# Input tiles turned in 32-blocks on VectorE and placed by DMA copies, low parts on GpSimd, maxima scores over 128 rows

## The chip, the cores and the metric

The kernel runs on one NeuronCore of a Trainium2 chip. The metric is device time in microseconds of one execution; the median of three runs is compared. The engines are TensorE (PE: matrix products into PSUM; PEld is its loading of the stationary operand), VectorE (DVE), ScalarE (ACT), GpSimd (POOL) and SyncE (SP), which here only issues DMAs. Each engine works through its own list in order, and semaphores tie the lists together. All DMAs of this kernel's main part are issued by SP.

## The reference

Cross-attention over 32 batches. Queries and context are both 512 x 512, there are 16 heads of 32.

```
qn  = layer_norm(q)  * g_q + b_q          # q = x[b],  512 x 512
kvn = layer_norm(kv) * g_k + b_k          # kv = ctx[b], 512 x 512
Q, K, V = qn @ Wq, kvn @ Wk, kvn @ Wv     # 16 heads of 32
attn = softmax(Q K^T / sqrt(32))
ctx  = attn V
out  = q + gelu(ctx @ Wo + bo)
```

## The kernel before

The accuracy is that of fp32, reached by splitting each operand of the large products into a high part (rounded to the type fp32r by a ScalarE copy) and a low part (what is left), and adding three products: high by high, high by low, low by high. So each 512-wide product of the projections takes 12 matrix instructions of 512 columns (L856), and one plan token of PE (`q`, `k`, `v`, `o`) stands for two of them.

A batch is worked in four steps; a step holds one unit, that is four heads. The loop `batch(b)` of every engine walks the same four steps, and what each engine does in a step, and in which order, is written out by hand in the table `ORDER` (`st*3` means three tokens `st`). In step s of batch b the kernel works on several units at once:

- `st` (L876): the 16 transposed score products of unit s, out of `k_stack` and `q_stack`; ScalarE turns each into `probs` by Exp (L563).
- `s` (L883): the 16 score products of unit s+1, only to find each row's maximum; VectorE reduces each (L706). They use the first 96 of the 128 rows of the stacks (`KROWS`), which hold high and low parts of Q and K one above the other. Rows 96 to 127 of `q_stack` take the negated maxima (`mx`, L617, which follows `m`, `mh`, `ml`), and those of `k_stack` a mask of heads, so that `st` subtracts the maxima.
- `q`, `k` (L856): the projections of unit s+2. ScalarE writes their high part and VectorE their low part into `q_nat` and `k_nat` (L594, L608, L688), and SP copies them into the stacks by `restack`: three DMAs of 256 KB each for q (`rq`) and three for k (`rk`), each from 128 partitions to 32 partitions. The stacks have two slots, so these copies wait on the semaphore `stack_used`, which the first matrix instruction of the first `pv` block after the last `st` raises. The first `s` of the next step waits for all six to have landed.
- `pv` (L903): two blocks of probabilities times V per step; `z` (L847): row sums over `probs`, after GpSimd has added the four chunks (`add`, L475, six per step); then VectorE's `zt zr zb cn` and the `split` of the context into `ctx_hl`.
- Once per batch: `v` and `o` projections, and the preparation of the next batch's eight input tiles (four of x, four of ctx, each 128 tokens x 512). A tile is loaded (`load`), its mean and variance are taken (`ln`, `la`, `lv`), ScalarE normalises it in place (`norm`, L584), PE transposes it with four 128 x 128 instructions into a PSUM bank (`x`, L943), ScalarE copies the high part to `xT` or `cT` (L588) and VectorE subtracts to get the low part (L686).

Before the first batch, a head (b = -1) prepares weights, biases and the first tiles.

## Time and profile before

| | |
|---|---|
| median of 3 runs | 3265.43 us (3265.21 to 3265.64) |
| profiled execution, its own time | 3262.8 us |
| its span | 3261.0 us |
| PE busy | 3230.8 us, 99% |
| DVE, ACT, POOL busy | 69%, 70%, 71% |
| DMA engines, mean busy share | about 60% |
| granted TensorE clock, mean | 0.998 |

The span is the time between first and last instruction of that one execution; the difference of 1.8 us to its own time lies around it. Of the page, the busy shares say who could bound, and the chain that ended last says who did: it is followed back from the last instruction through whatever released each step. The timeline of one engine shows single instructions, with the idle time in front of one in brackets.

### The profile page before, as it was taken

Reading aid. Unit: us, or ns where it says so; the run is one execution under the profiler, and the core shown is the slowest. Engines: PE = TensorE matmul, PEld = TensorE weight load, DVE = VectorE, ACT = ScalarE, POOL = GpSimd, SP = SyncE. Lnnn points to the kernel's source line nnn. Section 1 sums busy time; section 2 is a strip of 40 time slices with the busy share of each in tenths; the row PEclk is TensorE's granted clock in tenths of the full one; section 3 lists DMA queues with packets and bytes.
Section 4 is the critical chain, followed back from the end, with each engine's and each line's share of the span. In section 5 each row is a group of like instructions: output and inputs, shape, how many; then the busy total and the mean of one; then the engine's idle time right before and its main releaser. Section 6 shows DMA issues by size and latency. Waiting matters only on the chain.

```text
span 3261.0 us, 49855 instructions
## 1 busy us (share of the span) xinstructions
PE 3230.8 (99%) x16611; PEld 2135.1 (65%) x16611; DVE 2256.9 (69%) x4769; ACT 2280.3 (70%) x3985; POOL 2313.9 (71%) x1544
## 2 busy tenths in 40 slices
PE   8999999999999999999999999999999999999998
PEld 5566666666666666666666666666666666666664
DVE  6667667676676676666766766766667767667664
ACT  5677666777767777667767667776777676677765
POOL 3676776777677767777776677777767776777765
PEclk9999999999999999999999999999999999999999
DMA  5655656566556656565665566665656655666653
GB/s 142 87 108 107 108 104 116 91 111 107 107 104 104 111 107 107 104 118 89 111 109 106 105 102 111 109 104 104 120 86 112 107 107 107 100 111 108 105 79 76
DMA packets 186721, 343.02 MB, mean 105 GB/s; under 512 B 20561, under 2 KB 20577, under 8 KB 186466
## 3 DMA queue, kind: packets, MB, share of 16 engines
q1 hardware_dynamic: 186000, 339.03, 60.0%
q8 instruction: 134, 2.20, 0.3%
q10 hardware_dynamic: 466, 0.80, 0.2%
q14 instruction: 121, 0.99, 0.1%
HBM read 104.87 MB, written 33.55 MB: 42 GB/s over the span
## 4 chain that ended last, share of the span: by engine, by line
PE 97%; DVE 1%; ACT 1%; issue 1%; DMA 0%; POOL 0%; SPq 0%; ACTq 0%; POOLq 0%; DVEq 0%
PE gen L856 43%; PE score L883 16%; PE score L876 15%; PE ctx L903 14%; PE gen L847 4%; PE gen L943 4%; PE gen L965 1%; DVE maxes L706 1%; DMA k_stack<-k_nat 0%; ACT q_stack L617 0%; PE score L788 0%; ACT probs L563 0%; DVE stats L725 0%; PE gen L837 0%; POOL probs L475 0%
## 5 line engine op out<-in xcount | busy, mean ns | idle before, releaser
L475 POOL TENSOR_TENSOR probs<-probs 128x1024 f32<-128x1024 f32 x762 | 1800.3, 2392 | 287.8 <-PE ctx L903 281.6
L706 DVE TENSOR_REDUCE maxes<-score 128x1 f32<-128x512 f32 x2048 | 1294.9, 680 | 217.5 <-PE score L883 213.9
L563 ACT ACTIVATE probs<-score 128x512 f32<-128x512 f32 x2048 | 1090.2, 621 | 141.1 <-PE score L876 137.5
L883 PE MATMUL score<-k_stack,q_stack 96*128 96x512 f32 x2048 | 761.2, 413 | 3.3 <-DVE maxes L706 1.8
L876 PE MATMUL score<-q_stack,k_stack 128*128 128x512 f32 x2048 | 696.4, 406 | 6.6 <-ACT q_stack L617 6.5
L883 PEld LDWEIGHTS score<-k_stack,q_stack 96*128 96x128 f32 x2048 | 378.2, 188 | 221.3 <-ACT probs L563 83.6
L876 PEld LDWEIGHTS score<-q_stack,k_stack 128*128 128x128 f32 x2048 | 374.7, 188 | 199.9 <-DVE maxes L706 64.4
L903 PE MATMUL ctx<-probs,v_sb 128*32 128x512 f32 x4096 | 492.5, 598 | 0.0
L856 PE MATMUL gen<-cT,w_k 128*128 128x512 f32 x1536 | 461.7, 400 | 0.2 <-DVE q_nat L688 0.2
L856 PE MATMUL gen<-w_v,cT 128*128 128x512 f32 x1536 | 461.4, 395 | 0.0
L856 PE MATMUL gen<-xT,w_q 128*128 128x512 f32 x1536 | 447.9, 394 | 0.0
L856 PE MATMUL gen<-w_o,ctx_hl 128*128 128x512 f32 x1488 | 416.4, 396 | 0.0
L491 POOL TENSOR_TENSOR rstd<-var_eps,minus_half 128x1 f32<-128x1 f32 x256 | 140.5, 549 | 335.0 <-DVE neg_mean L737 333.1
L502 POOL TENSOR_TENSOR ctx_hl<-ctx_n,ctx_hl 128x512 fp32r<-128x512 f32 x128 | 164.2, 1283 | 290.4 <-ACT ctx_hl L569 290.4
L617 ACT ACTIVATE q_stack<-max_hl,chunk_mask 32x512 fp32r<-32x512 f32 x512 | 326.3, 706 | 42.3 <-DVE max_hl L771 41.5
L856 PEld LDWEIGHTS gen<-w_v,cT 128*128 128x128 f32 x1536 | 287.3, 189 | 84.1 <-issue 26.8
L856 PEld LDWEIGHTS gen<-xT,w_q 128*128 128x128 f32 x1536 | 288.5, 190 | 60.6
L856 PEld LDWEIGHTS gen<-cT,w_k 128*128 128x128 f32 x1536 | 287.5, 192 | 55.2 <-DVE q_nat L688 1.1
L688 DVE SCALAR_TENSOR_TENSOR k_nat<-gen,bias_k,k_nat 128x512 fp32r<-128x512 f32 x128 | 95.8, 748 | 318.0 <-ACT k_nat L608 318.0
L856 PEld LDWEIGHTS gen<-w_o,ctx_hl 128*128 128x128 f32 x1488 | 276.7, 189 | 57.3
L903 PEld LDWEIGHTS ctx<-probs,v_sb 128*32 128x32 f32 x4096 | 106.9, 109 | 233.8 <-issue 233.8
L574 ACT ACTIVATE v_sb<-gen 128x512 f32<-128x512 f32 x128 | 76.5, 598 | 255.1 <-PE gen L856 255.1
(89 smaller groups left out, 2765.4 us busy)
## 6 DMA issues: line engine op xcount, KB each, us to landing
k_stack<-k_nat SPq DMA_DIRECT2D x384, 256.0 KB, 7.6
q_stack<-q_nat SPq DMA_DIRECT2D x381, 256.0 KB, 5.6
tok<-in_x SPq DMA_DIRECT2D x132, 256.0 KB, 11.0
tok<-in_ctx SPq DMA_DIRECT2D x128, 256.0 KB, 12.0
res<-in_x SPq DMA_DIRECT2D x124, 256.0 KB, 2.7
out<-res SPq DMA_DIRECT2D x124, 256.0 KB, 2.1
probs<-in_L_xattn_Wq SPq DMA_DIRECT2D x1, 1024.0 KB, 8.2
probs<-in_L_xattn_Wk SPq DMA_DIRECT2D x1, 1024.0 KB, 10.4
```

The lines of the kernel that those rows point to most:

```text
L475: pool.tensor_tensor(probs[:, c + 1, heads], probs[:, c + 1, heads], probs[:, c, heads], ALU.add).then_inc(pool_added, 1)
L491: pool.tensor_tensor(rstd[:, n:n + 1], var_eps[:, n:n + 1], minus_half[:], ALU.pow).then_inc(ln_rstd, 1)
L502: pool.tensor_tensor(ctx_hl[:, 1, up], ctx_n[:], raw(ctx_hl[:, 0, up]), ALU.subtract).then_inc(ctx_split, 1)
L563: act.activation(probs[:, n, part, :], score_at(s, "st", i)[:], ACT.Exp, scale=SCALE).then_inc(exp_done, 1)
L617: act.activation(q_stack[SROW:P, u1 % 2, :, P * n:P * (n + 1)], raw(max_hl[SROW:P, :]).unsqueeze(1).to_broadcast([SHIFTS, HU, P]), ACT.Ide ...
L706: dve.tensor_reduce(maxes[:, u1 % 2, SROW + i:SROW + i + 1], score_at(s, "s", i)[:], AX_X, ALU.max, negate=True).then_inc(max_done, 1)
L847: mm = pe.matmul(bank[DH * j:DH * (j + 1), :], ones[:, 0:DH], probs[:, c, j, :], start=(i == 0), stop=(i == len(chunks) - 1))
L856: mm = pe.matmul(bank[:, :], stationary(hs, c), moving(hm, c), start=(i == 0), stop=(i == len(TERMS) * NC - 1))
L876: pe.matmul(score_bank(pe, b, s, "st", i)[:, :], k_stack[:, s % 2, part, P * n:P * (n + 1)], q_stack[:, s % 2, part, :], start=True, stop= ...
L883: pe.matmul(score_bank(pe, b, s, "s", i)[:, :], q_stack[0:KROWS, u1 % 2, n, P * part:P * (part + 1)], k_stack[0:KROWS, u1 % 2, n, :], star ...
L903: mm = pe.matmul(ctx_ps[DH * j:DH * (j + 1), :], v_sb[:, c, lo:lo + DH], probs[:, c, j, :], start=(c == 0), stop=(c == NC - 1))
L943: mm = pe.matmul(bank[:, P * c:P * (c + 1)], tok[:, n, P * c:P * (c + 1)], ident[:], start=True, stop=True, is_transpose=True)
```

## The change

The transposing of the input tiles leaves PE, for all batches but the first (whose tiles are still transposed on PE in the head). A tile is now loaded so that partition 32g+j holds token 128g+32t+j for tile t. VectorE turns it in blocks of 32 x 32 (`xt`, one 128 x 512 transpose per tile) into `turned_tok`; 16 DMAs of 64 KB for the four tiles of x and 16 for those of ctx (`xd`, four per token) copy the blocks into the low half of `xT` or `cT`, from 32 partitions to 32 partitions. ScalarE reads them there and writes the high half (`x`), and GpSimd subtracts in place to leave the low half (`x` in the list of GpSimd; on VectorE only in the head, `xl`). `tok` shrinks to four tiles.

The `s` products run over all 128 rows. For that rows 96 to 127 of the `q_stack` slot must be zero, so each `rq` now begins with a DMA of 256 KB of zeros from DRAM, which waits for `stack_used`; PE's first `s` waits for it too (`rows_cleared`).

All five tables of `ORDER` are new. The core of the diff (of the tables the lines of SP alone):

```diff
-        "load*8 rq rk store res",
-        "rq rk store res store",
-        "store first_res rk rq first_res",
-        "rq rk",
+        "load*5 rq rk",
+        "load*3 xd*4 rq rk store xd*2 res xd*2",
+        "store res store rk rq store first_res*2",
+        "rk rq",
...
+    zero_rows = nc.dram_tensor("zero_rows", (SHIFTS, HU * D), F32).ap()
...
-        tok = sb("tok", [P, 2 * NC, D])
+        tok = sb("tok", [P, NC, D])
+        turned_tok = sb("turned_tok", [P, NC, NC, NC, DH])
...
+                if (b, s) == (-1, 0):
+                    for i in range(2 * NC):
+                        load_tile(0, i)
                 if (b, s) == (-1, 1):
+                    sp.wait_ge(act_out_free, 1)
+                    sp.dma_start(zero_rows.rearrange("r (c n) -> (r c) n", n=D), act_out[:]).then_inc(zeros_stored, 16)
...
-                if valid(b - 1):
-                    wait(sp, full["x"], 8 * (b - 1) + i + 1)
-                src = x_v[NC * b + i] if i < NC else c_v[NC * b + i - NC]
-                sp.dma_start(tok[:, i, :], src).then_inc(tile_loaded[i], 16)
+                if known(b) and b == 1 and i < NC:
+                    wait(sp, full["x"], i + 1)
+                elif not known(b) or b > 0:
+                    wait(sp, tok_turned, 8 * b + i - 11)
+                src, n = (x_v, i) if i < NC else (c_v, i - NC)
+                if known(b) and b == 0:
+                    sp.dma_start(tile(b, i), src[n]).then_inc(tile_loaded[i], 16)
+                else:
+                    src = src.rearrange("(b n) p d -> b (n p) d", n=NC)[b]
+                    sp.dma_start(tile(b, i), src.rearrange("(g t j) d -> t g j d", g=NC, t=NC)[n]).then_inc(tile_loaded[i], 16)
+
+            def spread_tile(b, n):
+
+                which, g = "c" if n >= NC else "x", n % NC
+                if g == 0:
+                    wait(sp, tok_turned, 8 * (b - 1) + n + NC)
+                    if which == "x":
+                        wait(sp, full["q"], NU * b)
+                    else:
+                        wait(sp, full["k"], NU * b)
+                        wait(sp, full["v"], NC * b)
+                for m in range(NC):
+                    sp.dma_start(raw(xt[which][DH * m:DH * (m + 1), 1, g, :, :]),
+                                 turned_tok[DH * g:DH * (g + 1), m, :, :, :].rearrange("p c t j -> p c (t j)")
+                                 ).then_inc(x_landed[g], 16)
...
+                        if kind == "xd" and valid(b) and valid(b + 1):
+                            spread_tile(b + 1, n)
+                        if kind == "rq" and valid(b2):
+                            if known(b) and (b, s) == (-1, 2):
+                                sp.wait_ge(zeros_stored, 16)
+                            wait(sp, stack_used, NU * b2 + u2 + 1)
+                            sp.dma_start(raw(q_stack[SROW:P, u2 % 2, :, :]),
+                                         zero_rows.rearrange("r (c n) -> r c n", n=D)).then_inc(rows_cleared[u2 % 2], 16)
-                            wait(sp, stack_used, NU * b2 + u2 + 1)
                             if which == "q":
                                 restack(sp, u2, q_nat, q_stack, ((0, 0), (1, 0), (2, 1)), q_stacked)
                             else:
+                                wait(sp, stack_used, NU * b2 + u2 + 1)
...
+                        if kind == "x" and valid(b) and valid(b + 1):
+                            dst = xt["x" if n < NC else "c"]
+                            high, low = dst[:, 0, n % NC, :, :], dst[:, 1, n % NC, :, :]
+                            wait(pool, x_hi, 8 * (b + 1) + n + 1)
+                            pool.tensor_tensor(low, raw(low), raw(high), ALU.subtract).then_inc(free["x"], 1)
...
-                            wait(act, full["x"], 8 * (b + 1) + n + 1)
-                            act.activation(xt["x" if n < NC else "c"][:, 0, :, P * (n % NC):P * (n % NC + 1)],
-                                           gen_at("x", n)[:].rearrange("p (c n) -> p c n", c=NC),
-                                           ACT.Identity).then_inc(x_hi, 1)
+                            dst = xt["x" if n < NC else "c"]
+                            if known(b) and b == -1:
+                                wait(act, full["x"], n + 1)
+                                src = gen[n % NGEN][:].rearrange("p (c n) -> p c n", c=NC)
+                            else:
+                                wait(act, x_landed[n % NC], 64 * (2 * b + n // NC + 1))
+                                src = raw(dst[:, 1, n % NC, :, :])
+                            act.activation(dst[:, 0, n % NC, :, :], src, ACT.Identity).then_inc(x_hi, 1)
...
-                        if kind == "x" and valid(b + 1):
-                            src = xt["x" if n < NC else "c"]
-                            cols = slice(P * (n % NC), P * (n % NC + 1))
-                            wait(dve, x_hi, 8 * (b + 1) + n + 1)
-                            low_part(src[:, 1, :, cols], gen_at("x", n)[:].rearrange("p (c n) -> p c n", c=NC),
-                                     src[:, 0, :, cols], free["x"])
+                        if kind == "xl" and valid(b + 1) and known(b) and b == -1:
+                            dst = xt["x" if n < NC else "c"]
+                            wait(dve, x_hi, n + 1)
+                            low_part(dst[:, 1, n % NC, :, :], gen[n % NGEN][:].rearrange("p (c n) -> p c n", c=NC),
+                                     dst[:, 0, n % NC, :, :], free["x"])
+                        if kind == "xt" and valid(b) and valid(b + 1):
+                            if n % NC == 0:
+                                wait(dve, x_hi, 8 * (b + 1) + n)
+                            wait(dve, ln_done, 8 * (b + 1) + n + 1)
+                            dve.transpose(turned_tok[:, :, :, n % NC, :].rearrange("p m c j -> p c m j"),
+                                          tile(b + 1, n)).then_inc(tok_turned, 1)
...
+                                wait(pe, rows_cleared[u1 % 2], 16 * (NU // 2 * b1 + u1 // 2 + 1))
                                 wait(pe, k_stacked, 48 * (t1 + 1))
-                            pe.matmul(score_bank(pe, b, s, "s", i)[:, :], q_stack[0:KROWS, u1 % 2, n, P * part:P * (part + 1)],
-                                      k_stack[0:KROWS, u1 % 2, n, :], start=True, stop=True).then_inc(s_full, 1)
+                            pe.matmul(score_bank(pe, b, s, "s", i)[:, :], q_stack[:, u1 % 2, n, P * part:P * (part + 1)],
+                                      k_stack[:, u1 % 2, n, :], start=True, stop=True).then_inc(s_full, 1)
...
-                        if kind == "x" and valid(b + 1):
-                            bank = gen_bank(pe, b, "x", n)
-                            wait(pe, ln_done, 8 * (b + 1) + n + 1)
-                            for c in range(NC):
-                                mm = pe.matmul(bank[:, P * c:P * (c + 1)],
-                                               tok[:, n, P * c:P * (c + 1)], ident[:], start=True,
-                                               stop=True, is_transpose=True)
-                            mm.then_inc(full["x"], 1)
```

The order of SP from the end of step 3 on. Before, with q's copies ahead of k's, then the eight loads in step 0:

```order
L353 DMA q_stack<-q_nat 32x4x512 [waits stack_used,q_out_of_psum]
L353 DMA q_stack<-q_nat 32x4x512 x2
L353 DMA k_stack<-k_nat 32x4x512 [waits stack_used,k_out_of_psum]
L353 DMA k_stack<-k_nat 32x4x512 x2
L392 DMA tok<-in_x 128x512 [waits x_in_psum] x4
L392 DMA tok<-in_ctx 128x512 [waits x_in_psum] x4
```

And now (`L351` is the restack, `L448` the clearing, `L407` a load, `L420` an `xd` copy):

```order
L351 DMA k_stack<-k_nat 32x4x512 [waits stack_used,k_out_of_psum]
L351 DMA k_stack<-k_nat 32x4x512 x2
L448 DMA q_stack<-zero_rows 32x2048 [waits stack_used]
L351 DMA q_stack<-q_nat 32x4x512 [waits q_out_of_psum]
L351 DMA q_stack<-q_nat 32x4x512 x2
L407 DMA tok<-in_x 128x1x512 [waits tok_turned] x4
L407 DMA tok<-in_ctx 128x1x512 [waits tok_turned]
```

There are seven DMAs of 256 KB between `stack_used` and the first `s` where there were six; the last three loads move to step 1, ahead of the `xd` copies.

PE's list from step 3 into step 0, up to its first `s`. Before, the second `pv` of step 3 stands directly ahead of the first row, which is the maxima's transpose `m`; the first `s` is the row behind the last one here:

```order
L965 MATMUL gen<-ident,maxes 128x128 [waits max_copied,v_out_of_psum]
L856 MATMUL gen<-xT,w_q 128x512 [waits v_out_of_psum]
L856 MATMUL gen<-xT,w_q 128x512 x5
L856 MATMUL gen<-w_v,cT 128x512 [waits m_out_of_psum]
L856 MATMUL gen<-w_v,cT 128x512
L856 MATMUL gen<-xT,w_q 128x512 x4
L856 MATMUL gen<-w_v,cT 128x512 x2
L856 MATMUL gen<-xT,w_q 128x512 x2
L856 MATMUL gen<-w_v,cT 128x512 x2
L876 MATMUL score<-q_stack,k_stack 128x512 [waits max_done,shift_rows]
L876 MATMUL score<-q_stack,k_stack 128x512 [waits max_done]
L856 MATMUL gen<-w_v,cT 128x512 x4
```

And now (`L918` is a projection, `L946` an `s`, `L1019` the transpose `m`), with the second `pv` 23 matmuls of 512 columns ahead of `m`; the last row is the first `s`:

```order
L918 MATMUL gen<-w_v,cT 128x512 [waits q_out_of_psum]
L918 MATMUL gen<-w_v,cT 128x512
L946 MATMUL score<-k_stack,q_stack 128x512 [waits max_done]
L918 MATMUL gen<-w_v,cT 128x512 x6
L1019 MATMUL gen<-ident,maxes 128x128 [waits max_copied,z_out_of_psum]
L918 MATMUL gen<-w_v,cT 128x512 x4
L918 MATMUL gen<-xT,w_q 128x512 [waits v_out_of_psum]
L918 MATMUL gen<-xT,w_q 128x512 x5
L946 MATMUL score<-k_stack,q_stack 128x512 [waits k_stacked,max_done,rows_cleared1,q_stacked]
```

Between the first matrix instruction of the `pv` block that raises `stack_used` and the first `s` of the next step, PE's list held 53 instructions of 512 columns before and holds 42 now at this place.

The same stretch from step 1 to step 2, its end. Before:

```order
L965 MATMUL gen<-ident,maxes 128x128 [waits max_copied,x_out_of_psum]
L856 MATMUL gen<-w_o,ctx_hl 128x512 x8
L883 MATMUL score<-k_stack,q_stack 128x512 [waits max_done,k_stacked,q_stacked]
L856 MATMUL gen<-w_o,ctx_hl 128x512 x2
L883 MATMUL score<-k_stack,q_stack 128x512 [waits max_done]
```

And now:

```order
L1019 MATMUL gen<-ident,maxes 128x128 [waits max_copied,z_out_of_psum]
L918 MATMUL gen<-w_o,ctx_hl 128x512 x6
L918 MATMUL gen<-w_o,ctx_hl 128x512 [waits o_out_of_psum]
L918 MATMUL gen<-w_o,ctx_hl 128x512 x9
L946 MATMUL score<-k_stack,q_stack 128x512 [waits k_stacked,max_done,rows_cleared1,q_stacked]
```

Here the whole stretch from `pv` to `s` held 48 instructions of 512 columns, five groups of tile transposes and both `pv` blocks; now it holds 44 and both `pv` blocks. The other two stretches: from step 0 to step 1, 53 instructions, one `pv`, one `z` and three groups of transposes before, 43 and two `pv` now; from step 2 to step 3, 63, two `pv` and one `z` before, 48, one `pv` and one `z` now. Each stretch also holds one `m`.

## Rows read from the trace of the kernel before

**Rows 1.** The page: busy time of the engines, and chain by engine and line.

```profile
PE 3230.8 (99%) x16611; PEld 2135.1 (65%) x16611; DVE 2256.9 (69%) x4769; ACT 2280.3 (70%) x3985; POOL 2313.9 (71%) x1544
...
PE 97%; DVE 1%; ACT 1%; issue 1%; DMA 0%; POOL 0%; SPq 0%; ACTq 0%; POOLq 0%; DVEq 0%
```

**Rows 2.** The chain in order of time (start, length, what): one piece of each batch.

```profile
258.82 4.11 PE gen L856 x18
...
3152.42 4.11 PE gen L856 x18
```

**Rows 3.** Timeline of PE (start, length to the last end), around tile transposes, end of step 1.

```profile
1002.55 0.50 PE L883 MATMUL score<-k_stack,q_stack 96*128 96x512 f32 x1
1002.89 0.60 PE L943 MATMUL gen<-ident,tok 128*128 128x128 f32 x4
1003.25 0.71 PE L883 MATMUL score<-k_stack,q_stack 96*128 96x512 f32 x2
1003.80 1.55 PE L856 MATMUL gen<-w_o,ctx_hl 128*128 128x512 f32 x6
```

**Rows 4.** Timeline of PE: ends of a stretch with `st` and of one with `s`.

```profile
1137.01 0.62 PE L856 MATMUL gen<-cT,w_k 128*128 128x512 f32 x2
...
1141.11 0.63 PE L876 MATMUL score<-q_stack,k_stack 128*128 128x512 f32 x2
...
1148.45 0.63 PE L856 MATMUL gen<-w_v,cT 128*128 128x512 f32 x2
...
1154.28 0.62 PE L856 MATMUL gen<-w_v,cT 128*128 128x512 f32 x2
```

**Rows 5.** Groups by line and shape (count | busy us, mean ns | idle before): other engines.

```profile
L475 POOL TENSOR_TENSOR probs<-probs 128x1024 f32<-128x1024 f32 x762 | 1800.3, 2392 | 287.8 <-PE ctx L903 281.6 <-ACT probs L563 4.1 <-POOL probs L475 0.2
L502 POOL TENSOR_TENSOR ctx_hl<-ctx_n,ctx_hl 128x512 fp32r<-128x512 f32 x128 | 164.2, 1283 | 290.4 <-ACT ctx_hl L569 290.4
L717 DVE STREAM_TRANSPOSE ctx_n<-z_inv 128x512 f32<-128x512 f32 x128 | 90.3, 706 | 2.3
L686 DVE TENSOR_TENSOR xT<-gen,xT 128x512 fp32r<-128x512 f32 x128 | 88.0, 687 | 52.3 <-ACT xT L588 52.3
```

**Rows 6.** The chain of waits by waiter, for SP's queue (total us, times, longest).

```profile
SPq L304 <- PE ctx L903: 1443.6, 126, 27.4
```

**Rows 7.** One restack, step 3 to 0: `pv` and `s` on PE.

```profile
1146.03 1.92 PE L903 MATMUL ctx<-probs,v_sb 128*32 128x512 f32 x16
...
1162.32 0.40 PE L883 MATMUL score<-k_stack,q_stack 96*128 96x512 f32 x1
```

**Rows 8.** The same restack, its six DMAs by line L353, issue and landing.

```profile
L353 SPq DMA_DIRECT2D q_stack<-q_nat x3: 547/603/611, 1147.2 to 1148.4; - x3
L353 SPq DMA_DIRECT2D k_stack<-k_nat x3: 562/614/614, 1149.1 to 1150.4; - x3
...
DMA to landing us min/median/max: 4.2/7.7/11.0
```

**Rows 9.** Stretches (us, busy by engine, clock, DMA share, GB/s): restacking, loads, batch 0.

```profile
1150.00:1160.00 10.00, 10.00 (x53) 6.75 (x52) 6.81 (x13) 3.71 (x7) 8.06 (x5) 1.00 1.07 127
1162.00:1166.00 4.00, 4.00 (x22) 2.96 (x24) 3.36 (x10) 2.84 (x7) 3.52 (x2) 1.00 1.04 384
...
112.00:119.00 7.00, 5.57 (x13) 4.29 (x14) 3.75 (x7) 4.13 (x7) 3.81 (x3) 0.51 0.24 40
```

**Rows 10.** The chain in order of time, batch 0, step 1 to 2.

```profile
98.52 0.99 PE ctx L903 x5
...
102.77 11.01 DMA k_stack<-k_nat
...
113.87 1.19 PE score L883 x2
```

**Rows 11.** Timeline of PE: the two longest idle times, in brackets.

```profile
112.90 0.45 PE L965 MATMUL gen<-ident,maxes 128*128 128x128 f32 x1 [2.19 <-DVE maxes L765]
...
3228.73 4.97 PE L876 MATMUL score<-q_stack,k_stack 128*128 128x512 f32 x11 [3.42 <-ACT q_stack L617]
```

72 lines of the change are left out of this document (41 added, 31 removed), and 32 rows, old and new, of the table ORDER.

## The prediction

> **What bounds the kernel now.** I read the page's busy shares and chain first: PE is busy 99% of the span, and 97% of the chain is PE [rows 1]. So the kernel costs what PE's list costs. The chain in order of time then gives the length of a batch: the same piece of 18 matmuls ends step 3 at 258.82 and, 29 batches later, at 3152.42, so 99.8 us per batch [rows 2]. VectorE, ScalarE and GpSimd have 30% idle. Last I looked for what nearly bounds: what must happen between two places of PE's list. One such thing is long: SP waits 1443.6 us in all, 126 times, for `stack_used`, that is for the `pv` block of PE (L903) behind the last `st` [rows 6], and only then may the copies into the stacks start that the next step's first `s` needs.
>
> **That loop before.** At 1146.03 the `pv` block begins and at 1162.32 the first `s` of the next step [rows 7]. SP issues the first copy at 1147.15, 1.12 us behind the `pv`, and the sixth at 1150.4; it lands 11.0 us later, at 1161.4 [rows 8]. So the loop takes 1.12 + 14.25 = 15.4 us, and PE's work in it 16.3 us: 0.9 us to spare. Where the spare is gone it shows: in batch 0, which has no `o` work, the copies issued behind the `pv` at 98.52 land at 102.77 + 11.01 = 113.78, and `s` starts at 113.87, 0.09 us behind [rows 10]; that is 15.35 us again. The six copies are limited by the DMA engines: their share is full while they move 127 GB/s, which is 2.06 us for each 256 KB. The loads, which go to 128 partitions, move at 384 GB/s, 0.68 us for each [rows 9].
>
> **The change: what PE saves.** A group of four tile transposes runs from 1002.89 to 1003.25, 0.36 us, and the two `s` behind it take 0.55 us where two matmuls otherwise take 0.46: 0.45 us per group, eight per batch, **3.6 us per batch** [rows 3]. Running `s` over 128 rows: from 1148.45 to 1154.28 PE does 25 matmuls, about half of them `s`, at 0.233 us each; from 1137.01 to 1141.11 it does 18 with `st` in place of `s` at 0.228 [rows 4], the pace of the pure stretch (4.11/18) [rows 2]. If 96 rows are the reason, the 64 `s` and some 36 neighbours save 5 ns each, **0.5 us per batch**; if not, nothing, and a loss is excluded by `st`, which has 128 rows and is the faster one. I take 0.5. (The Trainium skill, "TensorE: Matmul & The Clock Gate", section on LDWEIGHTS, says that loading the stationary operand costs by its columns and not by its rows, so by it the 128 rows bring nothing; rows 4 speak mildly against that, and the sum would be 15 us higher by the page.) So PE's own list falls to 99.8 - 4.1 = 95.7 us per batch.
>
> **What the other engines get.** VectorE loses eight subtractions of 0.69 us and gets eight transposes of 0.71 [rows 5]: no change, 70 of 95.7 us. ScalarE keeps its eight copies. GpSimd gets eight subtractions of the form of L502, 1.28 us each [rows 5]: 72.3 + 10.3 = 82.6 us of 95.7, 86%. They stand between the `add`s of steps 1 and 2. In step 1, from the first `pv` on, GpSimd has six `add` of 2.39, one `x` and one `res_add` of 1.28: 16.9 us behind the end of that `pv`; PE reaches the `z` that waits for the last of them 19.2 us of its own work behind the start of the `pv`, 17.35 behind its end. That is cover of 0.4 us, thin, and the wait for copies below adds 2.6 to it. So nothing to pay; without that wait, up to 1 us per batch.
>
> **What the copies cost.** PE's work between the `pv` and the first `s`, counted with 0.229 us per matmul, 1.85 per `pv` block, 0.99 per `z`, 0.26 for `m` and 0.1 for each other change between products of 512 columns and these: step 0 to 1 holds 43 matmuls and two `pv`, 13.9 us; 1 to 2 holds 44 and two, 14.2; 2 to 3 holds 48, one `pv` and one `z`, 14.2; 3 to 0 holds 42 and two, 13.8. (The same count gives 16.3 for the 53 of before, as [rows 7] have it.) The loop takes 15.4 us as it stands, and now the clearing of rows 96 to 127 joins it: a seventh DMA of 256 KB in the same queue. Nothing in the trace goes from DRAM to 32 partitions. Its bounds are a load's 0.68 us (same source) and a restack's 2.06 (same width of destination) [rows 9]; it shares one feature with each, and I take the middle, 1.35. By the Trainium skill, "SBUF — State Buffer", section on the DMA port swizzle, 32 partitions reach half of the ports, at most 218 GB/s; that would be 1.2 us, an estimate from its figure, and the sum would be 18 us lower. The loop is then 1.12 + 14.25 + 1.35 + 0.09 = **16.8 us**, and PE waits at each first `s`: 2.9 + 2.6 + 2.6 + 3.0 = **11.1 us per batch**. What is behind `s` on PE waits too, and the next `pv` with it, so the wait is paid in every step and not caught up. With k the last to be ready, as in step 0, it is no better: its copies queue behind q's.
>
> The 16 `xd` copies of x are issued in step 1 once the last `q` is done, 7 us ahead of the `pv`, and ahead of `rq` in SP's list and in the queue. Each moves 64 KB between sets of 32 partitions: 0.51 us at 127 GB/s, 8.2 us in all, and SP needs 0.35 to 0.6 us for each issue. Their end lies between just ahead of the clearing's turn and 1.5 us behind: I take **0.7 us per batch**. Those of ctx are issued behind `rk` and have some 9 us until PE needs them: nothing. The loads (now behind a wait for VectorE's `xt`) land over 10 us ahead of their `ln`: nothing.
>
> **The sum.** 99.8 - 4.1 + 11.1 + 0.7 = 107.5 us per batch, 7.7 more. Thirty batches repeat in full; batch 0 waits there already and the last has three of its four loops, together half: 30.5 x 7.7 = 235. The profiled execution's 3262.8 + 235 = 3498; the median lies 2.6 above that execution: **3500 us**.
>
> **The rivals.** (a) **The clearing and the copies are hidden**: the extra DMA costs nothing (two bursts overlap in full). The six restacks alone still need 15.5 us, against 14.0 of PE's work: 1.5 x 4 - 4.1 = 1.9 more per batch, 3323 us. With the clearing at a load's 0.68 and no `xd` cost: 4.4 more, 3400 us. (b) **The clearing costs a restack's 2.06 and `xd` 1.5**: 107.5 + 2.8 + 0.8 = 111.1, so 3610 us. (c) **The clock falls as well.** PE waited 2.19 us without a drop just ahead of it, and 3.42 us at 3225 [rows 11]; in batch 0, among several waits, the grant over 112 to 119 us is 0.51, the level of 1.2 GHz, where 13 matmuls take 5.5 us in place of 3 [rows 9]. My waits of 2.6 to 3.0 us lie between. If each brings such a loss of 2.5 us, 10 us per batch more: 3800 us. (d) **The loop is covered, and the kernel is faster.** It decides at the loop's length: below 13.8 us no wait is left, below 15.0 the waits are smaller than the 4.1 us saved. Then 3262.8 - 31 x 4.1 + 2.6 = 3140 us, or some 30 more if GpSimd's thin cover at `z` costs its 1 us. For it speaks that all four stretches were set near 14 us, as though the copies landed within that; against it that six copies take 14.1 to 14.25 us in the places read and that the change adds bytes to them. (e) **The change doesn't do what it says**, so that PE's list is no shorter: excluded by its rows, in which L943 is gone behind the head.
>
> **How the numbers follow.** The forecast with its bounds, from 3400 to 3610, has 0.68; (a) with all hidden 0.07; (c) 0.08, of which the part with few drops lies below 3640; (d) 0.14; close to no change 0.03. The range of 3320 to 3640 leaves out (d) and most of (c). A measurement of this kernel tells about 0.2%, 6.5 us, from no change: faster 0.14, within that 0.03, slower 0.83.
>
> **What would show it.** Right: the page gives PE some 90% busy and the chain holds a tenth or more of DMA `k_stack` or `q_stack`; PE's first `s` (L946) of each step stands with 2.5 to 3 us idle in front; a batch is 107 us; the span between `pv` and first `s` is 16.8. Wrong: that span at 14 with no idle time, which would mean restack copies of 256 KB landing less than 1.8 us apart; DMA figures above 127 GB/s during restacks; or idle time that GpSimd's `add` releases at `z`. The saving is right if PE's busy time without idle falls by 4 us per batch, and the clock price is seen in the grant of each stretch.

## The result and the profile after

| | before | after |
|---|---|---|
| median of the runs | 3265.3 us | 3740.4 us (3735.8 to 3742.2) |
| ratio, with its 95% interval | | 1.1455 [1.1435, 1.1475] |
| span of the profiled execution | 3261.0 us | 3740.0 us (own time 3741.8) |
| one batch | 99.8 us | 115.0 us |

Slower, as forecast, but by 475 us where 235 were forecast, and outside the range that ended at 3640. The page of the kernel after has these lines where [rows 1] has those of before: busy time by engine, the clock granted to PE in 40 slices, and the chain by engine and by what it consists of.

```profile
PE 3321.9 (89%) x15619; PEld 2119.5 (57%) x15619; DVE 2294.6 (61%) x4769; ACT 2410.9 (64%) x4047; POOL 2619.7 (70%) x1792
...
PEclk9899999999999999999999999999999999999999
...
DMA 43%; PE 31%; DVE 9%; SPq 8%; ACT 6%; issue 4%; ACTq 0%; DVEq 0%; POOL 0%
DMA q_stack<-q_nat 17%; DMA tok<-in_ctx 14%; PE gen L918 11%; DMA k_stack<-k_nat 8%; PE score L946 7%; SPq L351 6%; PE ctx L966 6%; PE score L938 5%; DVE maxes L752 4%; DMA tok<-in_x 3%; ACT probs L606 2%; ACT q_stack L663 2%; SPq L448 1%; DVE ctx_n L757 1%; DVE turned_tok L794 1%
```

PE is no longer the chain: 43% of it are transfers, 25 points the restack copies (`q_stack`, `k_stack`) and 17 the token loads (`tok`), which had no place in the forecast. The chain of waits, by waiter, says for what PE stands (total us, times, longest):

```profile
PE score L946 <- DMA k_stack<-k_nat: 189.2, 64, 5.2
PE score L946 <- DMA q_stack<-q_nat: 157.4, 62, 3.5
PE score L938 <- DVE maxes L752: 26.5, 31, 1.8
PE score L938 <- ACT q_stack L663: 9.4, 10, 3.4
PE score L946 <- DVE maxes L752: 5.6, 8, 1.2
```

L946 is `s`, and only the first `s` of a unit waits for these copies. The two upper rows are 346.6 us in 31 batches, 11.2 us per batch: the forecast wait of 11.1 is there, in its place. So the loop that the forecast was about is real. What the forecast did not hold is seen in a stretch of 2900 us in the middle of each kernel (columns: stretch, length, busy us and count of PE, PEld, DVE, ACT, POOL, then the granted clock, the DMA engines' share, GB/s). First before, then after:

```profile
300.00:3200.00 2900.00, 2899.58 (x14992) 1924.87 (x14991) 2024.95 (x4261) 2053.98 (x3591) 2102.99 (x1380) 1.00 0.61 106
```

```profile
300.00:3200.00 2900.00, 2592.81 (x12226) 1661.12 (x12224) 1796.49 (x3751) 1897.01 (x3185) 2075.02 (x1415) 0.95 0.65 119
```

A batch has 516 matmul records before and 484 after, so the rows hold 29.05 and 25.26 batches, and a batch takes 99.8 and 114.8 us. PE is idle for 0.0 and 12.2 us of it, which leaves 102.6 us in which PE is busy after, where the forecast had its list at 95.7 us. The seven us between are the clue, and the clock of 0.95 says where to look: a tenth of the time is at half speed.

PE around one first `s` of step 3, with the idle time in front of it in brackets:

```profile
1542.13 0.50 PE L946 MATMUL score<-k_stack,q_stack 128*128 128x512 f32 x1 [1.89 <-DMA q_stack<-q_nat]
1542.47 1.55 PE L918 MATMUL gen<-xT,w_q 128*128 128x512 f32 x4
1543.83 1.48 PE L946 MATMUL score<-k_stack,q_stack 128*128 128x512 f32 x3
1545.24 2.43 PE L966 MATMUL ctx<-probs,v_sb 128*32 128x512 f32 x16
```

Behind the wait four matmuls take 1.36 us from start to start where four take 0.92 otherwise, three `s` 1.41 in place of 0.69, and the `pv` block 2.43 in place of 1.92 [rows 7]. The windows give the clock beside it:

```profile
1542.00:1545.00 3.00, 2.87 (x8) 2.00 (x8) 1.20 (x2) 0.69 (x1) 0.00 (x0) 0.65 0.34 112
1545.00:1547.00 2.00, 2.00 (x13) 0.52 (x16) 2.00 (x4) 0.03 (x1) 0.00 (x0) 0.67 0.00 0
1547.00:1550.00 3.00, 3.00 (x21) 1.75 (x17) 1.90 (x4) 0.57 (x1) 1.85 (x1) 1.00 0.72 124
```

For a while behind the wait the grant is 0.5, that is 1.2 GHz, and then again 1. From 300 to 3500 us there are 75 such stretches, 3.4 or 6.8 us long; before has none between 300 and 3200. Of the 114 waits of over 0.8 us at a first `s` in that time 73 go with one (they are 1.8 us and longer, 3.1 on average), 41 do not (at most 2.7 us, 2.0 on average). Of the 61 waits of 2.5 us and more 58 do, of the 53 shorter ones 15.

### Where a batch's time goes

To separate the terms I took every matmul's distance to the next one's start and set it against the median distance between the same kinds of neighbours in the kernel before. The medians' sum is the list; what exceeds it is a wait where the trace shows idle time (plus about 0.15 us of each wait that the modelled end of the matmul ahead hides), the lower clock where the grant is under 1, and else the rest, mostly `st` that wait a tenth of a us for a score bank. (The expectations of the first four runs were written ahead of this split and put the whole seven us down to the lower clock, as 7.1 us per batch; it is 4.5.) The kernel before was run again beside every group of runs, at 3263 to 3264 us. In us per batch, for all kernels of this study:

| kernel | median us | ratio to before [95%] | batch | list | waits | lower clock | rest |
|---|---|---|---|---|---|---|---|
| before | 3264 | 1 | 99.8 | 98.9 | 0.0 | 0.0 | 0.8 |
| after | 3740 | 1.146 [1.144, 1.148] | 115.0 | 95.4 | 13.4 | 4.5 | 1.6 |
| rows96 | 3597 | 1.102 [1.097, 1.107] | 110.6 | 95.4 | 11.3 | 1.8 | 2.1 |
| loads16 | 3672 | 1.125 [1.122, 1.128] | 112.8 | 95.4 | 11.6 | 4.1 | 1.7 |
| fill8 | 3724 | 1.141 [1.138, 1.144] | 114.4 | 103.0 | 8.7 | 1.2 | 1.4 |
| short | 3369 | 1.032 [1.029, 1.035] | 103.0 | 95.4 | 5.6 | 0.5 | 1.5 |
| loads16_fill8 | 3591 | 1.101 [1.096, 1.105] | 110.1 | 103.0 | 5.3 | 0.5 | 1.4 |
| short_loads16 | 3224 | 0.988 [0.985, 0.991] | 98.4 | 95.5 | 1.4 | 0.0 | 1.6 |
| rows96_loads16 | 3487 | 1.069 [1.065, 1.072] | 106.7 | 95.4 | 7.8 | 1.4 | 2.1 |
| rows96_loads16_later | 3517 | 1.078 [1.075, 1.081] | 107.6 | 95.7 | 7.8 | 2.0 | 2.2 |
| before128 | 3263 | 1.000 [0.999, 1.001] | 99.6 | 98.8 | 0.2 | 0.0 | 0.5 |
| before_late | 3664 | 1.123 [1.120, 1.125] | 112.6 | 98.9 | 9.2 | 3.7 | 0.8 |
| later2 | 3432 | 1.052 [1.050, 1.054] | 104.9 | 95.6 | 6.4 | 0.8 | 2.1 |
| xdsmall | 3742 | 1.147 [1.144, 1.149] | 114.9 | 95.5 | 13.1 | 4.7 | 1.6 |
| clearfirst_loads16 | 3524 | 1.080 [1.074, 1.086] | 107.8 | 95.4 | 8.7 | 2.1 | 1.7 |
| clearfirst_later | 3421 | 1.048 [1.045, 1.051] | 104.6 | 95.6 | 6.8 | 0.4 | 1.8 |

### The profile page after: what moved, and what is told of

Its sections match the earlier page's. It is cut to its first block, busy times and chain, and to the rows that moved or that the text cites. A ratio compares the mean times of both kernels' runs of the same rounds, so it can differ in the third digit from the quotient of the medians.

```text
span 3740.0 us, 49178 instructions
## 1 busy us (share of the span) xinstructions
PE 3321.9 (89%) x15619; PEld 2119.5 (57%) x15619; DVE 2294.6 (61%) x4769; ACT 2410.9 (64%) x4047; POOL 2619.7 (70%) x1792
## 4 chain that ended last, share of the span: by engine, by line
DMA 43%; PE 31%; DVE 9%; SPq 8%; ACT 6%; issue 4%; ACTq 0%; DVEq 0%; POOL 0%
DMA q_stack<-q_nat 17%; DMA tok<-in_ctx 14%; PE gen L918 11%; DMA k_stack<-k_nat 8%; PE score L946 7%; SPq L351 6%; PE ctx L966 6%; PE score L938 5%; DVE maxes L752 4%; DMA tok<-in_x 3%; ACT probs L606 2%; ACT q_stack L663 2%; SPq L448 1%; DVE ctx_n L757 1%; DVE turned_tok L794 1%
## 5 line engine op out<-in xcount | busy, mean ns | idle before, releaser
L752 DVE TENSOR_REDUCE maxes<-score 128x1 f32<-128x512 f32 x2048 | 1315.3, 681 | 868.5 <-PE score L946 863.8
L946 PE MATMUL score<-k_stack,q_stack 128*128 128x512 f32 x2048 | 795.0, 438 | 357.1 <-DMA k_stack<-k_nat 189.2
L938 PE MATMUL score<-q_stack,k_stack 128*128 128x512 f32 x2048 | 763.8, 425 | 38.6 <-DVE maxes L752 26.5
L946 PEld LDWEIGHTS score<-k_stack,q_stack 128*128 128x128 f32 x2048 | 402.6, 200 | 679.0 <-issue 299.4
L938 PEld LDWEIGHTS score<-q_stack,k_stack 128*128 128x128 f32 x2048 | 394.8, 198 | 271.8 <-ACT probs L606 92.3
L918 PE MATMUL gen<-xT,w_q 128*128 128x512 f32 x1536 | 496.8, 430 | 0.0
L918 PE MATMUL gen<-cT,w_k 128*128 128x512 f32 x1536 | 463.2, 404 | 0.0
L918 PE MATMUL gen<-w_v,cT 128*128 128x512 f32 x1536 | 443.3, 393 | 0.0
L918 PE MATMUL gen<-w_o,ctx_hl 128*128 128x512 f32 x1488 | 414.1, 399 | 2.7 <-DVE q_nat L730 2.6
L918 PEld LDWEIGHTS gen<-xT,w_q 128*128 128x128 f32 x1536 | 324.1, 211 | 72.5
L918 PEld LDWEIGHTS gen<-cT,w_k 128*128 128x128 f32 x1536 | 300.4, 197 | 67.0
L918 PEld LDWEIGHTS gen<-w_v,cT 128*128 128x128 f32 x1536 | 285.9, 188 | 59.4 <-issue 0.8
L918 PEld LDWEIGHTS gen<-w_o,ctx_hl 128*128 128x128 f32 x1488 | 273.3, 189 | 80.6 <-DVE q_nat L730 29.3
L730 DVE SCALAR_TENSOR_TENSOR k_nat<-gen,bias_k,k_nat 128x512 fp32r<-128x512 f32 x128 | 95.5, 746 | 249.8 <-ACT k_nat L654 248.2
L771 DVE BATCH_NORM_STATS2 stats<-tok 128x6 f32<-128x512 f32 x252 | 172.8, 686 | 74.1 <-DMA tok<-in_ctx 65.2
```

The lines of the kernel that those rows point to most:

```text
L730: dve.scalar_tensor_tensor(out=dst, in0=psum, scalar=bias, in1=raw(hi), op0=ALU.add, op1=ALU.subtract).then_inc(done, 1)
L752: dve.tensor_reduce(maxes[:, u1 % 2, SROW + i:SROW + i + 1], score_at(s, "s", i)[:], AX_X, ALU.max, negate=True).then_inc(max_done, 1)
L771: dve.bn_stats(stats[:, n, :], tile(b + 1, n)).then_inc(ln_stats, 1)
L918: mm = pe.matmul(bank[:, :], stationary(hs, c), moving(hm, c), start=(i == 0), stop=(i == len(TERMS) * NC - 1))
L938: pe.matmul(score_bank(pe, b, s, "st", i)[:, :], k_stack[:, s % 2, part, P * n:P * (n + 1)], q_stack[:, s % 2, part, :], start=True, stop= ...
L946: pe.matmul(score_bank(pe, b, s, "s", i)[:, :], q_stack[:, u1 % 2, n, P * part:P * (part + 1)], k_stack[:, u1 % 2, n, :], start=True, stop ...
```

## The experiments

The theory, A: the loop from `pv` over the burst of copies to the first `s` is longer than PE's work in it, and each wait there brings a stretch at the lower clock. The rivals: B, the token loads, which the trace of after shows at a quarter of their old speed; C, a lower clock from another cause; D, VectorE's own order; F, the copies of the turned tiles.

### One part undone, one suspect taken away

**Loads over all DMA engines.** The loads were the surprise of the trace. The loads of step 0 move once the burst issued ahead of them in step 3 is done; a window of that time:

```profile
1563.00:1570.00 7.00, 7.00 (x28) 4.57 (x27) 5.59 (x11) 3.20 (x6) 0.48 (x1) 0.76 0.26 102
```

They have 0.26 of the DMA engines busy and 102 GB/s, where loads before had the full share and 384 [rows 9]. The new order of tokens makes the outermost dimension of a load 4. (The Trainium skill, "DMA: Bandwidth & Descriptors", section on why a DMA increments its semaphore by 16, says that the number of engines is the largest one up to 16 that divides the outermost dimension, sizes of 1 left out, of both sides of a transfer; by that rule it is 4 of 16, and the share of 0.26 agrees.) The edit splits a load into four:

```diff
-                    sp.dma_start(tile(b, i), src.rearrange("(g t j) d -> t g j d", g=NC, t=NC)[n]).then_inc(tile_loaded[i], 16)
+                    src = src.rearrange("(g t j) d -> t g j d", g=NC, t=NC)[n]
+                    for g in range(NC):
+                        sp.dma_start(tok[DH * g:DH * (g + 1), n, :], src[g]).then_inc(tile_loaded[i], 16)
```

> The same token tiles are loaded with the same order of tokens, but each by four DMAs of 32 rows (64 KB) where the changed kernel has one whose outermost dimension is 4 and which moves at 100 GB/s. Theory A: the slow loads cost only what VectorE's statistics and the burst behind them lose: 0.8 us per batch at the scores that wait for VectorE's maxima, and about 0.5 us in the burst of step 0; against it stand 24 more issues of about 0.6 us on SP's queue. 113.5 to 115.5 us per batch, 3690 to 3755 us. Rival B (the slow loads are the main reason for the time): over 5 us per batch come back, under 3590 us.

3672 us, 2.2 us per batch less: between the two theories, below the range of A and far from B. The gain is where a load stands ahead of a burst. The burst of step 0 in after, with the clearing (L448) and the copies (L351), each with its issue times and its time to landing, and then the same in loads16:

```profile
L448 SPq DMA_DIRECT2D q_stack<-zero_rows x1: 338/338/338, 1577.2 to 1577.2; - x1
...
DMA to landing us min/median/max: 6.7/6.7/6.7
```

```profile
L351 SPq DMA_DIRECT2D q_stack<-q_nat x3: 605/612/622, 1577.6 to 1578.9; - x3
L351 SPq DMA_DIRECT2D k_stack<-k_nat x3: 547/605/611, 1583.0 to 1584.3; - x3
...
DMA to landing us min/median/max: 6.6/7.8/10.4
```

```profile
L351 SPq DMA_DIRECT2D q_stack<-q_nat x3: 557/603/617, 1086.5 to 1087.8; - x3
L351 SPq DMA_DIRECT2D k_stack<-k_nat x3: 548/604/609, 1092.0 to 1093.2; - x3
...
DMA to landing us min/median/max: 4.8/6.1/7.2
```

The longest of the copies takes 10.4 us behind a slow load and 7.2 without. Between 900 and 2000 us this burst lands 17.3 us behind its first issue on average in after (16.1 to 18.6, nine bursts) and 14.7 in loads16 (13.8 to 15.8, ten). Four issues for one have a price of their own: SP reaches the 16 `xd` copies of x later, and the burst behind them is first issued 2.4 us behind its `pv`, where in after it was 1.15. So in the means over 300 to 3200 us the wait at the first `s` of step 1 falls from 4.0 to 1.9 us and that of step 2 rises from 1.9 to 3.1; the 68 us are what is left of both. The second price of the slow loads is VectorE's: in the chain of after (start, length, what) VectorE, at the statistics of a tile, waits for a load of 13 us, and behind them, in VectorE's order, stands a `maxes` for which PE then waits.

```profile
1588.60 12.95 DMA tok<-in_ctx
...
1603.18 0.56 DVE maxes L752
1603.78 0.50 PE score L938
```

**The clearing and the 128 rows undone.**

```diff
-                            sp.dma_start(raw(q_stack[SROW:P, u2 % 2, :, :]),
-                                         zero_rows.rearrange("r (c n) -> r c n", n=D)).then_inc(rows_cleared[u2 % 2], 16)
...
-                                wait(pe, rows_cleared[u1 % 2], 16 * (NU // 2 * b1 + u1 // 2 + 1))
...
-                            pe.matmul(..., q_stack[:, u1 % 2, n, P * part:P * (part + 1)],
-                                      k_stack[:, u1 % 2, n, :], ...)
+                            pe.matmul(..., q_stack[0:KROWS, u1 % 2, n, P * part:P * (part + 1)],
+                                      k_stack[0:KROWS, u1 % 2, n, :], ...)
```

> One part undone: the scores for the maxima read 96 rows again and the clearing DMA of 256 KB is gone from each burst; everything else is as in the changed kernel (115.0 us per batch, of which 10.9 us are PE's waits for the restack at the first `s` of a unit and some 7.1 us are PE at the lower clock). Theory A (the loop pv, burst, first `s` is too long, and each wait also brings a stretch at the lower clock): a burst lands 1.3 us earlier, so the four waits fall from 10.9 to about 5.7 us per batch, the 64 scores cost 0.5 us more, and the low-clock loss falls with the waits, from 7.1 to 3 to 6 us: 107 to 109.5 us per batch, 3500 to 3575 us in all. If the low clock has nothing to do with the waits, it stays at 7.1: 110.3 us per batch, 3597 us. Rival B (the token loads, which now move at 100 GB/s, set when the burst lands and when VectorE gets to the maxima): the waits hardly move, over 112.5 us per batch, over 3660 us.

3597 us. The lower clock's part fell from 4.5 to 1.8 us, which speaks against C, but the waits fell by 2.1 only and not by 5.2. The chain of waits tells why:

```profile
PE score L943 <- issue: 94.0, 61, 3.4
PE score L943 <- DMA q_stack<-q_nat: 72.1, 62, 1.6
PE score L936 <- ACT q_stack L661: 46.9, 32, 3.4
PE score L936 <- DVE maxes L750: 39.9, 31, 3.0
PE score L943 <- DVE maxes L750: 34.0, 43, 1.5
```

The first two rows (the "issue" one stands where the copies of k end) are the loop, halved to 5.4 us per batch. The last three, 120.8 us or 3.9 per batch, are VectorE and what follows it, and stood at 1.3 in after (41.5 us in its last three rows). The 3597 is outside the range of A and is the very number of "waits alone"; the split shows that it is not that, since the clock's part did fall, but a gain in the loop and the clock of which a part was lost again behind VectorE.

**PE kept at work ahead of the wait.**

```diff
                             if i == 0:
+                                bank = score_bank(pe, b, s, "s", i)
+                                for _ in range(8):
+                                    pe.matmul(bank[:, :], w_hl["q"][:, 0, 0, 0:P], w_hl["q"][:, 0, 0, :], start=True, stop=True)
                                 wait(pe, q_stacked, 48 * (t1 + 1))
```

> The changed kernel with eight matmuls of 512 columns (1.8 us at the full clock) put on PE directly ahead of the wait at each unit's first `s`, into the bank that this `s` then overwrites; nothing else is touched, so the burst lands when it did. Theory A (the lower clock comes after PE has stood idle there): the wait of 2.7 us per unit shrinks to about 0.9, the granted clock stays at full speed, and the 7.1 us per batch at the lower clock go: 108 to 110 us per batch, 3525 to 3590 us, although PE does 7.4 us more work per batch. Rival C (the lower clock has another cause, as a limit on the work as such): the added work buys nothing, 115 to 117 us per batch, 3740 to 3800 us. Where the clock is full and the time is unchanged, the low clock was only ever inside time in which PE waited anyway, and the term has to be looked for elsewhere.

3724 us (3722 to 3726, against 3736 to 3742 of after). With 7.6 us per batch more work on PE the kernel is 16 us faster, the clock of the same 2900 us is 0.99 in place of 0.95, and the lower clock's part is 1.2. So the low stretches come from the standing still. But the time is far from the 3525 to 3590 of theory A:

```profile
PE score L938 <- DVE maxes L752: 42.4, 32, 2.7
PE score L949 <- DVE maxes L752: 38.0, 52, 1.7
PE score L938 <- ACT q_stack L663: 20.9, 24, 3.4
PE gen L918 <- DVE q_nat L730: 20.7, 21, 1.3
```

These four are 122 us, some 3.9 us per batch: VectorE was the next to be late, as in rows96.

**A shorter burst.** The third copy of each restack is 16 KB in place of 256, so this kernel leaves out a part of the computation.

```diff
-            for third, part in parts:
+            for i, (third, part) in enumerate(parts):
+                if i == 2 and short:
+                    eng.dma_start(raw(stack[DH * third:DH * (third + 1), u % 2, 0, 0:P]),
+                                  raw(nat[0:DH, part, 0:P])).then_inc(done, 16)
+                    continue
```

> In each restack the third of the three 256 KB copies is cut to a 16 KB piece (from the first batch on), so the rows 64 to 95 of the stacks keep old values: a part of the computation is left out. The burst lands about 4 us earlier, all else, the number of issues too, stays. Theory A: the loop is then about 13 us long against 13.9 us and more of PE's work, the waits at the first `s` go and the clock stays full: PE's list of 95.7 us per batch and 1 to 3 us for the rest, 97 to 99 us per batch, 3170 to 3240 us. Rival B (slow loads, copies of the turned tiles, GpSimd's and VectorE's order bound the batch beside the loop): over 102 us per batch, over 3340 us.

3369 us: by far the largest gain, 12 us per batch, for 4 us of burst. The loop is the cause of most of it. But 103.0 is not 97 to 99, it is in the range of rival B, and what is left is the same group of waits, 77 us in the two longest rows:

```profile
PE score L942 <- DVE maxes L756: 43.9, 32, 2.9
PE gen L922 <- DVE q_nat L734: 33.0, 30, 2.0
```

**The copies of the turned tiles**, cut from 64 KB to 4 KB.

```diff
-                    sp.dma_start(raw(xt[which][DH * m:DH * (m + 1), 1, g, :, :]),
-                                 turned_tok[DH * g:DH * (g + 1), m, :, :, :].rearrange("p c t j -> p c (t j)")
+                    sp.dma_start(raw(xt[which][DH * m:DH * (m + 1), 1, g, 0, 0:DH]),
+                                 turned_tok[DH * g:DH * (g + 1), m, 0, 0, :]
```

> The changed kernel with each of the 32 copies per batch that spread the turned tiles cut from 64 KB to 4 KB; their number and places in SP's queue stay, and a part of the computation is left out. Theory A (the bytes of these copies cost little, since SP issues them in about 0.6 us each whatever they carry): 0 to 1 us per batch less, 3705 to 3745 us. Rival F (they hold up the bursts and the loads on the DMA engines): over 2.5 us per batch, under 3665 us.

3742 us: their bytes cost nothing that shows in the time, and F is out as far as the bytes go. What their issues cost was not tried alone; the late burst in loads16 shows 1.3 us per batch for them once the loads take more issues too.

### Are the late VectorE and the slow loads one thing?

Four kernels now shared the leftover, waits behind VectorE. Either it is held by tiles that land late (A with B as a second term), or it is late by its own order (D).

> The restacks with their third copy cut to 16 KB (a part of the computation is left out; alone 3369 us, 103.0 us per batch against PE's list of 95.4, the rest being 5.6 us of waits, nearly all behind VectorE's maxima and low parts) together with the loads by four DMAs of 32 rows. Theory A (these waits are those of VectorE behind tiles that land late): 97.5 to 99.5 us per batch, 3190 to 3255 us. Rival D (VectorE's own order is the bound once the burst is short): 101.5 us per batch or more, over 3310 us.

> Loads by four DMAs of 32 rows each (that alone measured 3672 us: per batch 112.8 us, of which 11.6 are waits and 4.1 what the lower clock adds to PE's instructions) together with the eight matmuls (1.8 us) ahead of the wait at each unit's first `s` (alone 3724 us: the lower clock's part fell from 4.5 to 1.2 us per batch, but waits for VectorE's maxima, 1.2 us per batch before, took some 3 us instead). Theory A (the filled kernel did not gain because VectorE, held by the statistics of tiles that land late, was late next): without the slow loads the clock's part comes out, 109 to 110.5 us per batch, 3550 to 3600 us. Rival D (VectorE is late for a reason of its own, the order or the amount of its work): no better than 112 us per batch, 3640 us or more.

> Two parts undone: scores over 96 rows without the clearing DMA (alone 3597 us, 110.6 us per batch, of which 7.4 us at the first `s` and some 4 us behind VectorE), and the loads by four DMAs of 32 rows (alone 3672 us). Theory A (the two are separate terms: the burst is 1.3 us shorter in each of four loops, and VectorE is no longer held by tiles that land late): 106.5 to 108.5 us per batch, 3470 to 3540 us. Rival D (VectorE is late by its own order): 110 us per batch, 3580 us. What then is left over before (99.8 us) is the loop, 15.4 us against 13.8 to 14.2 us of PE's work.

All three fell into the range of A: 3224, 3591 and 3487 us. The loads at full width give 145 us beside the short burst, 133 beside the filled wait, 110 beside 96 rows, and 68 alone. So the slow loads cost more the less of the other causes is there, and D is out as the reason of these waits. In short_loads16 the rows of VectorE are gone from the chain of waits; what is left of it beside the start and the end of the kernel:

```profile
PE score L952 <- DMA k_stack<-k_nat: 11.6, 15, 5.2
PE score L944 <- ACT probs L612: 6.8, 31, 0.3
```

And in loads16_fill8 the stretch of 2900 us has 13598 matmuls at 516 per batch, 110.0 us, at the full clock:

```profile
300.00:3200.00 2900.00, 2787.31 (x13598) 1815.62 (x13597) 1864.08 (x3926) 1981.27 (x3328) 2172.80 (x1484) 1.00 0.71 125
```

Against loads16 (112.8) PE does 7.6 us more work, of which 6.3 lie in what was waiting, and loses 3.6 less to the clock: the filling costs 1.3 us net and gives back 3.6.

### The first `s` later

With 96 rows and full loads a loop is 15.4 us, and PE's work in it 13.8 to 14.2. So the first `s` of steps 0, 1 and 2 was put about 1.9 us later in PE's order; the core of it:

```diff
-        "q*3 s*3 q*2 s q st s st z st*3 ...
+        "q*6 st s*3 st s*2 z st*3 ...
-        "q o q o q o st*3 o st q st*3 q s st q st s*2 st k st k s k*2 s z ...
+        "q o q o q o st*3 o st q st*3 q st q st*3 k s k s*2 k s k s z ...
-        "o*8 s o s*3 st q*3 st s st*4 s st z ...
+        "o*9 st q*3 s st s st s*2 st*2 s st*2 s z ...
```

> As rows96_loads16, and in PE's order the first `s` of steps 0, 1 and 2 stands 1.9, 1.9 and 2.1 us later, by matmuls of q, k, o and `st` put ahead of it; step 3 stays, since its `pv`, v_sb and VectorE's sixteen maxima leave no room. Three of the four loops then have 15.7 to 16.3 us of PE's work against the 15.4 us that the burst takes. Theory A: these three waits and their low clock go, some 5 us per batch against rows96_loads16: 101 to 103.5 us per batch, 3300 to 3380 us. Rival E (the maxima that come later make `m`, the shift rows and the next `st` late, so that a wait only moves): 105 us per batch or more, over 3420 us.

3517 us, rival E: a wait only moved. Most of it is a single one per batch, 107.3 us in 33 waits for ScalarE. PE's rows and ScalarE's rows at that place:

```profile
1066.08 0.66 PE L945 MATMUL score<-k_stack,q_stack 96*128 96x512 f32 x1 [3.09 <-ACT probs L606]
```

```profile
1057.11 4.52 ACT L606 ACTIVATE probs<-score 128x512 f32<-128x512 f32 x9
1061.64 1.28 ACT L623 ACT_TABLE_LOAD   x1
...
1064.13 1.28 ACT L606 ACT_TABLE_LOAD   x1
```

ScalarE takes nine `st`, then does `gelu` and `q` with two table loads, 3.8 us; my order had put more `st` than nine ahead of `s`, and they hold the banks that `s` needs. With nine ahead, and k matmuls in the place of the others (`... q st q st k*2 s*2 st s k st s k s z ...`):

> The later first `s` once more (96 rows, loads by four DMAs of 32 rows), with step 1's order mended: there ten `st` had stood ahead of the first `s`, while ScalarE takes nine and then turns to `gelu`, `q` and two loads of its function tables, so that `s` waited 3.4 us per batch for a score bank that ScalarE still had to read. Now nine `st` stand ahead and k matmuls take the place of the others. Theory A: that wait goes, and of the 107.6 us per batch 102.5 to 104.5 are left, 3350 to 3420 us, less than the 3487 us of the same kernel with the changed kernel's order. Rival E (the wait moves on once more): 106 us or more, over 3450 us.

3432 us, 104.9 us per batch, just outside the 102.5 to 104.5 of theory A and clearly on its side. The wait of 3 us is down to 1.2 (38.6 us in 32 waits), the lower clock's part is down to 0.8, and some 3.3 us per batch behind ScalarE, VectorE and score banks stay. Moving the first `s` by hand pays, but each move meets the next bound within 2 us.

### Parts of the change in the kernel before

**The burst put off, and nothing else.**

```diff
+                        if kind == first_of_burst and valid(b2):
+                            wait(sp, stack_used, NU * b2 + u2 + 1)
+                            for i in range(2):
+                                sp.dma_start(tick_rows, x_v[0][0:1, :]).then_inc(ticks, 16)
+                                wait(sp, ticks, 16 * (2 * (NU * b2 + u2) + i + 1))
```

> The kernel before, with each unit's burst of restack copies put off by two small DMAs (one row of 512 numbers between two places in DRAM) that SP issues and waits for one after the other, once the stack is free; nothing else is changed. At some 2 us for each round the burst lands 4 us later than it did, against 0.9 us spare, so that each first `s` finds a wait of about 3 us, as in the changed kernel. Theory A (the wait and the low clock behind it are a matter of the loop alone): 4 x 3.2 = 13 us of waits and 4 to 5 us by the lower clock per batch, 116 to 119 us per batch, 3760 to 3850 us. If the lower clock in the changed kernel came from something else in it (GpSimd, the copies of the turned tiles, the scores over 128 rows): waits alone, 112.5 us per batch, 3650 us.

3664 us: near the number for "waits alone" and not in the range of A, and yet the split is A's: 9.2 us of waits and 3.7 us by a lower clock (0.96 over the middle 2900 us). The waits are smaller than the 13 us expected because the loops of before are not all alike: over 300 to 3200 us the copies land 1.0, 1.5, 2.2 and 4.1 us ahead of the first `s` on average in the four steps. My forecast had read one step and taken its "0.9 us to spare" for all. Of the waits here 4.9 us per batch are at a first `s` (151.6 us in 75 waits); most of the others are behind VectorE and ScalarE (65.8 and 45.3 us). What the run shows of the clock is the important part: a kernel that has no part of the change, only a late burst, gets the same low stretches, 0.4 us lost for each us of waiting (in after 0.34, and 0.16 in rows96, whose waits are shorter).

**The clearing and the 128 rows in the kernel before.** The same lines as in the change, in before's order.

> One part of the change alone in the kernel before: scores for the maxima over all 128 rows, and the DMA of 256 KB that clears rows 96 to 127 ahead of each burst; PE's transposes of the tokens, its order and the token loads stay. The loop there has 16.3 us of PE's work against 15.4 us. Theory A: the burst lands 1.3 us later, which is 0.4 us more than the 0.9 us that are spare, so waits of 0.4 to 0.6 us stand at four first `s` per batch, the scores cost 0.5 us less, such short waits leave the clock full or nearly so: 100.5 to 102.5 us per batch, 3290 to 3350 us. If waits this short bring the lower clock as well: 105 us per batch, 3430 us. If the clearing is hidden in the spare time: 3250 us.

3263 us, 1.000 [0.999, 1.001]: neither the 1.35 us nor the waits are seen. Its bursts are 0.2 to 0.3 us longer than before's in the three steps where the clearing stands ahead of them and 1.0 us in the one where it stands inside, and there before had 4.1 us to spare; so nothing is left to wait for. This pointed to the next question.

### What the clearing costs

In step 0 and 1 the clearing stands at the head of the burst, in 2 and 3 behind the three copies of k. Its place was tried:

```diff
-                        if kind == "rq" and valid(b2):
+                        if kind == next(k for k, _n, _p in PLAN["sp"][s] if k in ("rq", "rk")) and valid(b2):
```

> Scores over 128 rows and loads by four DMAs of 32 rows (that alone: 3672 us, 112.8 us per batch), and in steps 2 and 3, where the copies of k go first, the clearing DMA now stands ahead of them, as it does in steps 0 and 1 ahead of q. Theory G (the clearing costs 1.2 us where it stands inside a burst, and next to nothing at its head, where the copies behind it land 1.8 to 1.9 us apart and not 2.06): two bursts per batch land 1.1 us earlier, 110 to 111.3 us per batch with some low clock less, 3585 to 3625 us. Theory H (as forecast: 1.35 us in every burst wherever it stands): unchanged, 112.5 to 113 us per batch, 3665 to 3680 us.

> The same, with PE's order of the kernel whose first `s` comes later (3432 us with 96 rows and no clearing, 104.9 us per batch). Theory G: a clearing at the head of every burst costs 0 to 0.4 us in the loops, and 128 rows give back 0.5 us per batch, so the two ways differ little: 104.5 to 106 us per batch, 3420 to 3465 us. Theory H: each loop that still waits is 1.35 us longer, 107 to 109 us per batch, 3495 to 3560 us.

3524 us, 107.8 us per batch: theory G's direction, and well below its range: 5.0 us per batch less than loads16, 2.9 of them waits and 2.0 the lower clock. In the order with room for the burst the clearing is then free, as G has it (its range was 3420 to 3465): 3421 us against 3432 with no clearing and 96 rows. One burst with k first in after, its copies, between which the clearing is issued at 957.2:

```profile
L351 SPq DMA_DIRECT2D k_stack<-k_nat x3: 609/611/612, 955.3 to 956.6; - x3
L351 SPq DMA_DIRECT2D q_stack<-q_nat x3: 547/603/603, 957.9 to 959.1; - x3
...
DMA to landing us min/median/max: 4.2/8.0/11.7
```

and one in clearfirst_loads16, the clearing issued ahead of them at 1005.0:

```profile
L351 SPq DMA_DIRECT2D k_stack<-k_nat x3: 605/610/612, 1005.4 to 1006.7; - x3
L351 SPq DMA_DIRECT2D q_stack<-q_nat x3: 634/650/678, 1007.3 to 1008.8; - x3
...
DMA to landing us min/median/max: 4.9/8.2/11.1
```

From the first issue to the last landing it is 15.5 us (955.3 to 959.1 + 11.7) in the one and 14.9 (1005.0 to 1008.8 + 11.1) in the other. Between 900 and 2000 us the bursts with k first take 15.5 us in nearly every case in after, and all those of clearfirst_loads16 13.1 to 15.5, 14.4 on average, where six copies without a clearing take 14.25 [rows 8]. With the clearing at the head the copies land 1.7 to 2.0 us apart and not 2.06. Why a transfer from DRAM at the head makes those behind it faster, no run here tells.

## Why the prediction was wrong

The direction and the loop as mechanism were right, the size was not: two terms were put at nothing. By its steps:

- **PE's list, 95.7 us.** Nearly right: 95.4 by the medians and 1.6 of small waits, 97.0 in all where before has 99.7. short_loads16, the one kernel with nearly no waits, has a batch of 98.4, 1.4 below before; the other 3 us are 1.4 of waits and 1.6 of small ones. The 0.5 us for 128 rows is borne out: the rest is 2.1 to 2.2 where `s` has 96 rows on the changed order, and 1.4 to 1.8 with 128; before128 is 0.2 us per batch below before.
- **GpSimd.** Right: the `z` that wait for it cost 3.6 us in seven waits in the whole execution of short_loads16.
- **Waits of 11.1 us at the first `s`.** The sum is right, 11.2, partly by luck: from step 0 to 1, 1 to 2, 2 to 3 and 3 to 0 PE stood 4.0, 1.9, 2.4 and 2.7 us on average over 300 to 3200 us, where 2.9, 2.6, 2.6 and 3.0 were forecast. Two errors cancel. **The clearing at 1.35 us in every burst** is 1.2 where it stands inside the burst and 0.2 to 0.3 at the head (before128; 0.15 in clearfirst_loads16). And the burst of step 0 was 2.5 us longer by the slow loads.
- **`xd` at 0.7 us.** The bytes cost nothing (xdsmall), and in after the burst behind them is issued 1.15 us behind its `pv`, as elsewhere. In loads16 it is 2.4: their issues on SP are the price, and it falls due when SP gets to them later.
- **"The loads ... land over 10 us ahead of their `ln`: nothing."** This step failed. I took their 0.68 us from [rows 9] although the diff gives them a new order of dimensions. They move at 102 GB/s, hold up the burst of step 0 and VectorE, and cost 2.2 us per batch as the kernel stands, 68 us in all, and up to 145 us once the rest is repaired.
- **The clock.** The larger failure. The sum had no term for it, though the forecast itself expected PE to stand for 2.6 to 3.0 us four times per batch; it was left to rival (c), at 10 us per batch and a chance of 0.08. I read the rows as even evidence, and that was a misreading. The wait of 2.19 us ends at 112.90 [rows 11], and the stretch of [rows 9] at a grant of 0.51 runs from 112 to 119: the drop goes with that wait. The one longer wait behind the head ends at 3228.73, and it has its drop as well: the grant there is 0.5 from 3228.5 to 3231.9 (the window around it is shown below this list). So both waits of over 2 us that before has behind its first 10 us went with a drop, and four waits of 2.6 to 3.0 us per batch could not be put at nothing. (One more drop, from 37.0 to 40.5 us in the head, has no wait ahead of it.) Measured: 4.5 us per batch, 137 us, behind two of three waits and not behind each, and 1.7 us for each low stretch in place of 2.5. Rival (c) had it behind every wait, and its 3800 is 60 us above what came.

The kernel before around its wait of 3.42 us:

```profile
3220.00:3236.00 16.00, 11.45 (x46) 5.33 (x47) 5.46 (x10) 8.65 (x17) 13.97 (x6) 0.89 0.00 1
```

By the columns of the table the forecast's 107.5 is a list of 95.7 with its small waits, 11.8 of waits and no lower clock; measured are 97.0, 13.4 and 4.5, together 114.9 of the batch's 115.0. So 4.5 of the 7.5 us that were missing are the clock's, 1.6 are waits, most of them behind VectorE and its late tiles, and 1.3 are in the list and its small waits. 30.5 x 7.5 is 230 of the 240 us that were missing; some 10 us lie at the kernel's two ends.

Of the signs that the prediction named, PE at 89%, DMA in the chain and the idle time at L946 came as it said; the batch of 107 us did not, and PE's busy time per batch did not fall by 4 us but rose from 99.8 to 102.6, since the lower clock is in it.

None of the kernels that compute everything is faster than before. The best of those made from the change, clearfirst_later, is 4.8% slower. Work taken off PE is of use here only as far as the loops have room: before had 1.0, 1.5, 2.2 and 4.1 us of it in the four.

## What to carry to other kernels

A wait of 2 to 3 us of PE is not paid with its length alone; here, in after and before_late, a third to two fifths came on top, because PE ran at 1.2 GHz for a while behind it, so a forecast with such waits needs a term for the clock, and eight useless matmuls per wait were worth more than they cost (16 us alone, 81 beside the loads at full width). When a transfer's access pattern changes, its old duration is void: look at what its outermost dimension has become, and then at everything that is queued behind it. And where a cause is undone and the gain stays away, look in the chain of waits for the one that was second: here each of two repairs gave 68 and 16 us alone and 149 together.

## What was not expected of the hardware

- A DRAM-to-SBUF transfer of 256 KB with an outermost dimension of 4 had 0.26 of the DMA engines busy and moved 102 GB/s; the same bytes in four pieces of 32 rows went with the full share but at 228 GB/s (loads16, 1073 to 1076 us), not at the 384 of a load of 128 rows.
- A transfer of 256 KB from DRAM to 32 partitions at the head of a burst of six copies from 128 to 32 partitions cost next to nothing: 14.4 us on average with it in clearfirst_loads16, 14.25 without, and 0.2 to 0.3 us in before128, while inside the burst it cost 1.0 to 1.2 us. There it lands 1.3 to 1.5 us behind the copy ahead, 175 to 200 GB/s, which stays under the 218 GB/s that the Trainium skill, "SBUF — State Buffer", section on the DMA port swizzle, gives for 32 partitions; the copies from SBUF to SBUF, also to 32 partitions, reached 127 GB/s alone and some 140 behind a clearing (1.85 us apart in the median).
- PE's grant fell to 0.5 at the end of waits of 1.8 us and more, for 3.4 or 6.8 us: with 58 of the 61 waits of 2.5 us and more in after, and with 15 of the 53 of 0.8 to 2.5 us.
